# Eight graph convolutions on one core: the two chunks of a node pair moved by one transfer per stream

## Chip, cores and metric

The kernel runs on one core of a Trainium2 chip. The metric is the device time of one execution in microseconds (us). The engines are PE (matmul; PEld is its weight load), DVE (vector), ACT (scalar), POOL and SP; a trailing q (SPq, ACTq) marks work that the engine's sequencer does, such as issuing a transfer.

## What is computed

A chain of graph layers on 100,000 nodes of 128 features and 50,000 edges sorted by destination. Three GCN layers come first, then two EVE layers, two SAGE layers and one GAT layer; there are normalisations between them. All are gathers over the edges, a sum (or max) for each destination, and a matmul of every node row. The GCN layer, cut from the reference:

```python
loop = jnp.arange(N, dtype=src.dtype)
src2, dst2 = jnp.concatenate([src, loop]), jnp.concatenate([dst, loop])
deg = jax.ops.segment_sum(ew2, dst2, num_segments=N)
dinv = jnp.where(deg > 0, jax.lax.rsqrt(jnp.maximum(deg, 1e-12)), 0.0)
norm = dinv[src2] * ew2 * dinv[dst2]
msg = norm[:, None] * (x @ W)[src2]
out = jax.ops.segment_sum(msg, dst2, num_segments=N) + b
h = out + x0          # then relu (not after the last) and a batch norm over the nodes
```

An EVE layer is `x @ wself.T + eve @ weve.T + bias` with `eve` from the segment's max and min; a SAGE layer is `agg @ W_l.T + b + x @ W_r.T` with the segment's mean. The second layer of each ends in a residual sum with x0 and a layer norm.

## The kernel before

Node rows are cut into 98 chunks of 1024 rows (`CH`), 8 consecutive rows on each of 128 partitions (`T` = 8), so that a chunk is 512 KB with 4 KB on a partition. Two chunks make a node pair: 49 pairs, the last of 1024 and 672 rows. Edges are cut into chunks of 1024 too: 24 edge pairs and a rest.

The program is a row of phases with a barrier between them: constants and indices, then `Degrees` (trace time 89 to 893 us: adds up the degrees, writes rows scaled by dinv and fills the first table of sums with bias rows), the convolutions m0, m1, m2 (GCN, 893 to 5934), a normalisation of the nodes (5934 to 6499), m4 and m5 (EVE, 6499 to 10039), m6 and m7 (SAGE, 10039 to 13216), and the GAT layer (13216 to the end). m5 and m7 are the ones that add x0 and end in the layer norm.

In a convolution every engine runs its own copy of one order, `merged_sweep` (line 902): the unit of an edge pair, then the units of those node pairs whose destinations are complete, mostly two behind each edge pair (24 such bursts, with a first and a second unit). POOL does nothing but the edges' side: 392 indirect gathers (line 1070) and 392 indirect scatters (line 1078) in a convolution.

A node unit in class `Conv`:

- `load_nodes` (lines 1146 to 1171, SP): for every stream (the rows y, where there is one x0, and last the sums that the edges scattered) the two chunks, each by its own transfer into its own buffer with a semaphore of its own. The y transfer of chunk b waits until half b of the previous pair has been transposed and copied, the others until half b of their buffer has been used. There is one buffer for each chunk of a pair, so the next pair's chunk goes where this one's was. Two fills of the next table of sums with bias rows follow, from one row in SBUF.
- `turn_nodes` (PE, line 1187): 16 transposes, two banks a chunk, behind `have`, the wait for the chunk's y. `turned_to_sbuf` (ACT, line 1220) copies the four banks, `multiply_nodes` (PE, line 1205) multiplies them.
- `LinearNodes.vector` (EVE and SAGE; DVE, line 1772) adds the sums to the products into z, behind `have` for that chunk's sums. `GcnNodes.vector` adds x0 and sums into res_b (line 1669) and then the scaled products (line 1683) into acc.
- `finish_scalar` (ACT) makes the output of the previous pair, o or y1 (lines 1808, 759 and in GCN 1651); each chunk waits in `out_free` for the store of the same buffer a pair earlier. `store_before` and `store_pair` (line 1250) issue the two stores from ACT.

`Degrees` loads (line 1967), scales (ACT line 2062, DVE line 2095) and stores (ACT line 2070) in the same way, chunk by chunk, with the two fills (line 2074) behind the stores on ACT.

Of the kernel before, what the change touches and what calls it, by code (L numbers as in the profile page):

```python
# [82 lines left out]
def node_rows(t, c, sh):  # L83

    if isinstance(c, int) and c == sh.node_chunks - 1:
        part = t[0:sh.last_nodes, :]
    elif isinstance(c, int):
        part = t[sh.n - CH * (c + 1):sh.n - CH * c, :]
    else:
        part = t[bass.ds((sh.n - CH) - c * CH, CH), :]  # L90
    return part.rearrange("(p j) f -> p j f", j=T)

# [906 lines left out]
class Conv(Phase):  # L999
# [10 lines left out]
    def __enter__(self):  # L1010
# [20 lines left out]
        self.buf = {n: [self.sb(f"in_{n}{b}", [P, T, D]) for b in range(2)] for n in self.streams}  # L1031
        self.landed = {n: self.pair(f"landed_{n}") for n in self.streams}
# [4 lines left out]
        self.stored = self.pair("stored")  # L1037
# [108 lines left out]
    def load_nodes(self, sp, m, scattered):  # L1146


        for name in sorted(self.streams, key=lambda name: name == "sums"):
            for b in range(2):  # L1150
                c = m * 2 + b
                if name == "y":
                    sp.wait_ge(self.nodes_turned, 2 * m + b + 1)
                    sp.sem_inc(self.gate, 1)
                if name in self.used:
                    sp.wait_ge(self.used[name], 2 * m + b + 1)
                    sp.sem_inc(self.gate, 1)
                if name == "sums" and b == 0:
                    for s, n in enumerate(scattered):
                        if not isinstance(n, int) or n > 0:  # L1160
                            sp.wait_ge(self.scattered[s], 16 * T * n)
                            sp.sem_inc(self.gate, 1)
                sp.dma_start(self.buf[name][b][0:self.sh.rows(c), :, :],
                             node_rows(self.streams[name], c, self.sh)).then_inc(self.landed[name][b], 16)

        if self.fill_table is not None:
            for b in range(2):
                c = m * 2 + b
                n = self.sh.rows(c)
                sp.dma_start(node_rows(self.fill_table, c, self.sh),  # L1170
                             spread_slots(self.fill_row[0:n, :], [n, T, D])).then_inc(self.filled, 16)

    def all_filled(self, sp):
        if self.fill_table is not None:
            sp.wait_ge(self.filled, 16 * self.sh.node_chunks)

    def have(self, eng, name, m, b):
        eng.wait_ge(self.landed[name][b], 16 * m + 16)

    def turn_nodes(self, pe, m):  # L1180
        for i in range(4):
            n = self.sh.rows(m * 2 + i // 2)
            if i % 2 == 0:
                self.have(pe, "y", m, i // 2)
            pe.wait_ge(self.n_out_read, 4 * m + i + 1)
            for t in range(H):
                mm = pe.transpose(self.n_bank[i][:, t * P:t * P + n], self.buf["y"][i // 2][0:n, H * (i % 2) + t, :],  # L1187
                                  self.k["ident"][0:n, 0:n])
            mm.then_inc(self.n_turned, 1)

    def multiply_nodes(self, pe, m, weight, between=None, add=None):
        for i in range(4):
# [4 lines left out]
            if add:  # L1197
                if i % 2 == 0:
                    self.have(pe, add, m, i // 2)
# [35 lines left out]
    def store_before(self, act, m, out):  # L1235
        act.wait_ge(self.finished, 2 * m + 2)
        act.sem_inc(self.gate, 1)
        if isinstance(m, int):
            self.store_pair(act, m - 1, out)
        else:  # L1240
            with act.If(0 < m):
                self.store_pair(act, (m - 1).with_bounds(min_val=0), out)
            with act.Else():
                for b in range(2):
                    act.sem_inc(self.stored[b], 16)

    def store_pair(self, act, m, out):
        for b in range(2):
            c = m * 2 + b
            act.dma_start(node_rows(self.out_dram, c, self.sh), out[b][0:self.sh.rows(c), :, 0:D]).then_inc(self.stored[b], 16)  # L1250

    def out_free(self, eng, m, b):
        eng.wait_ge(self.stored[b], 16 * m + 16)

    def all_stored(self, eng):
        for b in range(2):
            eng.wait_ge(self.stored[b], 16 * self.sh.node_pairs + 32)
# [328 lines left out]
class GcnNodes:  # L1586
# [3 lines left out]
    def __init__(self, ph, no, scale_shift, next_scale_shift, as_rows):  # L1590
# [10 lines left out]
        self.y1 = [ph.sb(f"y1{b}", [P, T, D + 1]) for b in range(2)]  # L1601
# [7 lines left out]
        self.grants = [(ph.nodes_turned, 2)] + [(ph.used[n], 2) for n in ph.used] + [(s, 16) for s in ph.stored]  # L1609
# [35 lines left out]
    def finish_scalar(self, act, m):  # L1645
        ph = self.ph
        for b in range(2):
            n = ph.sh.rows((m - 1) * 2 + b)
            act.wait_ge(self.acc_done, 2 * m + b + 1)
            ph.out_free(act, m, b)  # L1650
            act.wait_ge(self.gram_done, 2 * m + 1)
            act.activation(self.y1[b][0:n, :, 0:D], self.acc[b][0:n, :, :], ACT.Copy if self.last else ACT.Relu).then_inc(ph.finished, 1)
        ph.store_before(act, m, self.y1)
# [4 lines left out]
    def vector(self, dve, m, scattered):  # L1658
        ph, k = self.ph, self.ph.k
        dve.wait_ge(ph.n_out_read, 4 * m + 4)  # L1660
        for b in range(2):
# [4 lines left out]
            ph.have(dve, self.res, m, b)  # L1666
            ph.have(dve, "sums", m, b)
# [63 lines left out]
class LinearNodes:  # L1731


    def __init__(self, ph, weight, finish):
        self.ph, self.weight, self.finish = ph, weight, finish
        self.z, self.o = ([ph.sb(f"{n}{b}", [P, T, D]) for b in range(2)] for n in ("z", "o"))
# [3 lines left out]
        self.grants = [(ph.nodes_turned, 2)] + [(ph.used[n], 2) for n in ph.used] + [(s, 16) for s in ph.stored]  # L1740
# [19 lines left out]
    def vector(self, dve, m, scattered):  # L1760
# [3 lines left out]
        for i in range(4):  # L1764
# [3 lines left out]
            ph.multiplied_node(dve, m, i)  # L1768
            if i % 2 == 0:
                ph.have(dve, "sums", m, b)  # L1770
# [25 lines left out]
    def finish_scalar(self, act, m):  # L1796
# [4 lines left out]
        for b in range(2):  # L1801
            n = ph.sh.rows((m - 1) * 2 + b)
            ph.out_free(act, m, b)
# [5 lines left out]
        ph.store_before(act, m, self.o)  # L1809
# [65 lines left out]
class Degrees(Phase):  # L1875
# [9 lines left out]
    def __enter__(self):  # L1885
# [9 lines left out]
        self.x = [self.sb(f"x{b}", [P, T, D]) for b in range(2)]  # L1895
        self.xs = [self.sb(f"xs{b}", [P, T, WIDE]) for b in range(2)]
# [9 lines left out]
        self.x_in, self.deg_in, self.stored = self.pair("x_in"), self.pair("deg_in"), self.pair("stored")  # L1906
# [6 lines left out]
    def grant(self, pool):  # L1913
        pool.sem_inc(self.deg_read, 1)
        for b in range(2):
            pool.sem_inc(self.low_scaled[b], 1)
            pool.sem_inc(self.high_scaled[b], 1)
            pool.sem_inc(self.stored[b], 16)
# [48 lines left out]
    def load(self, sp, m, scattered):  # L1967
# [6 lines left out]
        sp.sem_inc(self.gate, 1)  # L1974
        for b in range(2):
            c = m * 2 + b
            sp.dma_start(self.deg[0:sh.rows(c), b, :].unsqueeze(2), node_rows(self.dram["degree"], c, sh)).then_inc(self.deg_in[b], 16)
        for b in range(2):
            c = m * 2 + b
# [4 lines left out]
            sp.dma_start(self.x[b][0:sh.rows(c), :, :], node_rows(self.x_dram, c, sh)).then_inc(self.x_in[b], 16)  # L1984
# [67 lines left out]
    def node_scalar(self, act, m, scattered):  # L2052
# [4 lines left out]
        for b in range(2):  # L2057
            n = sh.rows(m * 2 + b)
            act.wait_ge(self.x_in[b], 16 * m + 16)
            act.wait_ge(self.stored[b], 16 * m + 16)  # L2060
# [3 lines left out]
        for b in range(2):  # L2064
            c = m * 2 + b
# [4 lines left out]
            act.dma_start(node_rows(self.out_dram, c, sh), self.xs[b][0:sh.rows(c), :, :]).then_inc(self.stored[b], 16)  # L2070
        for b in range(2):
            c = m * 2 + b
            n = sh.rows(c)
            act.dma_start(node_rows(self.fill_table, c, sh), spread_slots(self.fill_row[0:n, :], [n, T, D])).then_inc(self.filled, 16)

    def node_vector(self, dve, m, scattered):
        sh, k = self.sh, self.k
        for b in range(2):
            dve.wait_ge(self.deg_in[b], 16 * m + 16)
# [10 lines left out]
        for b in range(2):  # L2090
            n = sh.rows(m * 2 + b)
            dve.wait_ge(self.x_in[b], 16 * m + 16)
            dve.wait_ge(self.stored[b], 16 * m + 16)
# [8 lines left out]
def degrees(nc, k, dram, sh, x, out, fill):  # L2102
    with Degrees(nc, k, dram, sh, x, out, fill) as ph:
        with nc.Block() as block:
# [15 lines left out]
            def _(act):  # L2120
                act.wait_ge(ph.constants_set, 4)
                merged_sweep(act, k, sh, lambda *u: ph.scalar(act, *u), lambda *u: ph.node_scalar(act, *u), first_behind=3)
                for b in range(2):
                    act.wait_ge(ph.stored[b], 16 * sh.node_pairs + 16)
                act.wait_ge(ph.filled, 16 * sh.node_chunks)
# [566 lines left out]
```

## Time and profile before

| | us |
|---|---|
| median of 3 runs | 10869.92 |
| lowest and highest run | 10861.84, 10874.02 |
| the profiled execution, first to last instruction | 15443.7 |
| Degrees, in the trace | 804 |
| m0, m1, m2 (GCN), in the trace | 1665, 1690, 1686 |
| m4, m5 (EVE), in the trace | 1656, 1884 |
| m6, m7 (SAGE), in the trace | 1488, 1689 |

The profiled execution is 42% longer than the runs, which the prediction comes back to. A row of the timeline gives the start from the beginning of the span, the duration, the engine, the line and operation, the output and inputs, and for several alike in a row their count; in brackets the engine's idle time ahead of it and what ended it. Under --lines a group's row gives the count, the busy time, the mean of one, and its idle time by what ended it. The names leave buffer numbers out; m stands for all seven convolutions.

### The profile page before, as it was taken

What the parts mean: (1) busy time and instruction counts of PE and PEld (TensorE: products, weight loads), DVE (VectorE), ACT (ScalarE), POOL (GpSimd) and SP (SyncE); (2) the same over time, 40 slices, a digit from 0 to 9 for tenths busy, and PEclk for the clock granted to TensorE, in tenths of its full rate; (3) what the DMA queues carried; (4) which work ended last, traced back from release to release, by engine and by line L of the source; (5) the groups of instructions that cost most, each with busy time, mean ns of one, the idle gap of its engine ahead of it and who ended that gap; (6) DMA issues with size and microseconds to landing.
All of it is one profiled execution on the core that took longest, in us unless ns stands there. A gap on an engine that the chain in (4) does not pass through costs nothing. (4 is left out here: it accounts for less than half of the span.)

```text
span 15443.7 us, 165743 instructions
## 1 busy us (share of the span) xinstructions
PE 7253.9 (47%) x36946; PEld 5501.8 (36%) x36947; DVE 6203.1 (40%) x16108; ACT 4646.1 (30%) x8631; POOL 7180.1 (46%) x7582
## 2 busy tenths in 40 slices
PE   1024544454534448854455555533334445445553
PEld 0024444444534444333333333323333333223332
DVE  3333433343434335522222333322223333378887
ACT  1111111111211114422222333412223333266676
POOL 4654444444454441144444444355554444557663
PEclk9987777777767779977777777866666667667776
DMA  6965554666656667644444444545555555233333
GB/s 164 209 154 171 172 167 148 205 200 194 202 176 198 193 194 255 235 142 158 143 166 143 162 160 159 177 144 173 168 171 170 183 177 192 81 104 119 114 114 100
DMA packets 1864962, 2570.76 MB, mean 166 GB/s; under 512 B 255901, under 2 KB 1369141, under 8 KB 1864662
## 3 DMA queue, kind: packets, MB, share of 16 engines
q1 hardware_dynamic: 1134168, 1627.20, 32.9%
q10 hardware_dynamic: 504726, 564.87, 11.2%
q0 software_dynamic: 225792, 375.94, 8.7%
q14 instruction: 216, 1.77, 0.0%
q8 instruction: 60, 0.98, 0.0%
HBM read 1499.55 MB, written 1129.98 MB: 170 GB/s over the span
## 5 line engine op out<-in xcount | busy, mean ns | idle before, releaser
L1078 POOL DMA_INDIRECT sums_gcn<-m_result,m_idx x1176 | 1162.8, 989 | 2311.9 <-DVE m_result L1399 1952.8
L1220 ACT ACTIVATE m_nodeT<-m_n_bank 128x512 f32<-128x512 f32 x980 | 544.3, 597 | 4220.6 <-remote 2400.8
L1626 PE MATMUL m_gram<-m_y 128*128 128x129 f32 (+1 forms) x4800 | 900.6, 336 | 1765.6 <-issue 1462.9
L1683 DVE SCALAR_TENSOR_TENSOR m_acc<-m_n_bank,m_scales,m_res_b 128x128 f32<-128x128 f32 (+1 forms) x2352 | 644.9, 343 | 2569.6 <-remote 1864.2
L1078 POOL DMA_INDIRECT sums_eve<-m_result,m_idx x784 | 762.7, 973 | 1696.8 <-DVE m_result L1515 1470.9
L1187 PE MATMUL m_n_bank<-k_ident,m_in_y 128*128 128x128 f32 x5488 | 895.6, 321 | 1310.0 <-DVE m_z L1772 826.9
L1772 DVE TENSOR_TENSOR m_z<-m_n_bank,m_in_sums 128x512 f32<-128x512 f32 (+1 forms) x784 | 511.9, 687 | 2412.8 <-remote 1300.2
L1626 PEld LDWEIGHTS m_gram<-m_y 128*128 128x128 f32 (+1 forms) x4800 | 801.2, 245 | 1845.4 <-issue 1523.6
L1078 POOL DMA_INDIRECT sums_sage<-m_result,m_idx x784 | 762.7, 973 | 1375.9 <-DVE m_result L1399 1134.3
L1070 POOL DMA_INDIRECT m_rows<-node_rows_a,m_idx x1176 | 1124.4, 956 | 358.5 <-issue 338.1
L1187 PEld LDWEIGHTS m_n_bank<-k_ident,m_in_y 128*128 128x128 f32 x5488 | 754.1, 168 | 1437.8 <-DVE m_z L1772 902.7
L1222 ACT ACTIVATE m_nodeT<-m_n_bank,k_bn 128x512 f32<-128x512 f32 x392 | 285.9, 775 | 1931.9 <-PE m_n_bank L1187 1404.6
L1070 POOL DMA_INDIRECT m_rows<-node_rows_b,m_idx x784 | 749.6, 956 | 247.4 <-issue 231.5
L1205 PE MATMUL m_n_bank<-k_gcn,m_nodeT 128*128 128x128 f32 (+1 forms) x4704 | 696.0, 308 | 95.1 <-issue 64.2
L1201 PE MATMUL m_n_bank<-m_in_x,k_ident 128*128 128x512 f32 (+1 forms) x784 | 476.3, 693 | 558.9 <-ACT m_nodeT L1220 408.0
L1119 PE MATMUL m_e_turn<-k_ident,m_rows 128*128 128x128 f32 x2744 | 488.8, 309 | 483.1 <-DVE m_sums L1582 224.9
L2215 POOL DMA_INDIRECT sums_gat<-g_result,g_idx x392 | 441.0, 1125 | 578.3 <-DVE g_result L2509 465.8
L1205 PEld LDWEIGHTS m_n_bank<-k_gcn,m_nodeT 128*128 128x128 f32 (+1 forms) x4704 | 663.6, 223 | 117.2 <-issue 83.7
L1205 PE MATMUL m_n_bank<-k_self,m_nodeT 128*128 128x128 f32 x3136 | 472.3, 310 | 456.5 <-ACT m_nodeT L1220 396.3
L1205 PEld LDWEIGHTS m_n_bank<-k_self,m_nodeT 128*128 128x128 f32 x3136 | 464.0, 225 | 579.5 <-ACT m_nodeT L1220 405.6
L759 ACT ACTIVATE m_o<-m_z,m_ln_shift,m_ln_scale 128x128 f32<-128x128 f32 x1600 | 626.5, 479 | 94.0 <-DMA node_rows_c<-m_o 46.6
L1129 PE MATMUL m_e_out<-k_gcn,m_sums 128*128 128x128 f32 x2352 | 393.1, 319 | 514.0 <-DVE m_result L1399 423.6
(302 smaller groups left out, 17415.1 us busy)
## 6 DMA issues: line engine op xcount, KB each, us to landing
m_in_sums<-sums_gcn SPq DMA_DIRECT2D x291, 512.0 KB
m_in_y<-node_rows_a SPq DMA_DIRECT2D x291, 512.0 KB
sums_gcn<-k_gcn_b SPq DMA_DIRECT2D x194, 512.0 KB
node_rows_a<-m_y ACTq DMA_DIRECT2D x194, 512.0 KB
m_in_x<-in_x_dram SPq DMA_DIRECT2D x194, 512.0 KB
m_in_y<-node_rows_b SPq DMA_DIRECT2D x194, 512.0 KB
sums_eve<-k_eve_b SPq DMA_DIRECT2D x194, 512.0 KB
m_in_sums<-sums_eve SPq DMA_DIRECT2D x194, 512.0 KB
```

Of the source, the lines that this page charges most:

```text
L759: ins = act.activation(out[0:n, j, :], z[0:n, j, :], ACT.Identity, bias=self.shift[copy][0:n, at:at + 1], scale=self.scale[copy][0:n, at:a ...
L1070: pool.indirect_dma_start(self.rows[b][:, t, :], None, self.table[:, :], bass.IndirectOffsetOnAxis(self.idx[s][:, t:t + 1], 0)).then_inc(s ...
L1078: pool.indirect_dma_start(self.node_sums[:, :], bass.IndirectOffsetOnAxis(self.idx[s][:, T + t:T + t + 1], 0), self.result[b][:, t, :], No ...
L1119: mm = pe.transpose(bank[:, n * P:(n + 1) * P], self.rows[b][:, H * (i % 2) + n, 0:D], self.k["ident"][:, :])
L1187: mm = pe.transpose(self.n_bank[i][:, t * P:t * P + n], self.buf["y"][i // 2][0:n, H * (i % 2) + t, :], self.k["ident"][0:n, 0:n])
L1201: mm = pe.matmul(self.n_bank[i][0:n, :], self.k["ident"][0:n, 0:n], half.rearrange("p t f -> p (t f)"), start=True, stop=False)
L1205: mm = pe.matmul(self.n_bank[i][0:n, t * D:(t + 1) * D], self.nodeT[:, i, t * P:t * P + n], weight[:, :], start=not add, stop=not add or t ...
L1220: act.activation(out, src, ACT.Copy).then_inc(self.n_turn_read, 1)
L1626: mm = pe.matmul(self.gram[:, 0:D + 1], self.y1[b][0:rows[b], t, 0:D], self.y1[b][0:rows[b], t, :], start=False, stop=False, skip_group_ch ...
L1683: ins = dve.scalar_tensor_tensor(out=self.acc[b][0:n, tt, :], in0=ph.node_out(i, n)[:, t, :], scalar=self.scales[b][0:n, tt:tt + 1], in1=s ...
L1772: dve.tensor_tensor(self.z[b][0:n, half, :], ph.node_out(i, n), ph.buf["sums"][b][0:n, half, :], ALU.add).then_inc(ph.n_out_read, 1)
L2215: pool.indirect_dma_start(self.node_sums[:, :], bass.IndirectOffsetOnAxis(self.idx[s][:, T + t:T + t + 1], 0), self.result[b][:, t, :], No ...
```

## The change

The two chunk buffers of every stream, of the outputs and of the degree phase become halves of one tile with 16 slots. A pair's 2048 rows lie 16 to a partition (8 KB), and one transfer with one semaphore moves them: loads, fills and stores. The load waits until both halves are free; the readers wait once, for the whole pair; an output's buffer is free when the whole pair is stored. The last pair, with its shorter chunk, keeps two transfers a stream. The same rows are moved, the loops and the order on each engine stay, and the normalisation and the GAT phase aren't touched. In `Degrees` it is the same with the loads of degree and x, the store and the fill. The diff, cut to its core:

```diff
+def pair_rows_of(t, m, sh):
+    at = sh.n - 2 * CH * (m + 1) if isinstance(m, int) else bass.ds((sh.n - 2 * CH) - m * (2 * CH), 2 * CH)
+    part = t[at:at + 2 * CH, :] if isinstance(m, int) else t[at, :]
+    return part.rearrange("(p j) f -> p j f", j=2 * T)
...
-        self.buf = {n: [self.sb(f"in_{n}{b}", [P, T, D]) for b in range(2)] for n in self.streams}
-        self.landed = {n: self.pair(f"landed_{n}") for n in self.streams}
+        self.both = {n: self.sb(f"in_{n}", [P, 2 * T, D]) for n in self.streams}
+        self.buf = {n: [t[:, b * T:(b + 1) * T, :] for b in range(2)] for n, t in self.both.items()}
+        self.landed = {n: self.sem(f"landed_{n}") for n in self.streams}
...
-            for b in range(2):
-                c = m * 2 + b
-                if name == "y":
-                    sp.wait_ge(self.nodes_turned, 2 * m + b + 1)
-                    sp.sem_inc(self.gate, 1)
-                if name in self.used:
-                    sp.wait_ge(self.used[name], 2 * m + b + 1)
-                    sp.sem_inc(self.gate, 1)
...
-                sp.dma_start(self.buf[name][b][0:self.sh.rows(c), :, :],
-                             node_rows(self.streams[name], c, self.sh)).then_inc(self.landed[name][b], 16)
+            if name == "y":
+                sp.wait_ge(self.nodes_turned, 2 * m + 2)
+                sp.sem_inc(self.gate, 1)
+            if name in self.used:
+                sp.wait_ge(self.used[name], 2 * m + 2)
+                sp.sem_inc(self.gate, 1)
...
+            else:
+                sp.dma_start(self.both[name][:, :, :], pair_rows_of(self.streams[name], m, self.sh)).then_inc(self.landed[name], 16)
...
-    def have(self, eng, name, m, b):
-        eng.wait_ge(self.landed[name][b], 16 * m + 16)
+    def have(self, eng, name, m):
+        eng.wait_ge(self.landed[name], 16 * m + (32 if is_last(m, self.sh) else 16))
...
     def store_pair(self, act, m, out):
-        for b in range(2):
-            c = m * 2 + b
-            act.dma_start(node_rows(self.out_dram, c, self.sh), out[b][0:self.sh.rows(c), :, 0:D]).then_inc(self.stored[b], 16)
-
-    def out_free(self, eng, m, b):
-        eng.wait_ge(self.stored[b], 16 * m + 16)
+        if is_last(m, self.sh):
...
+        else:
+            act.dma_start(pair_rows_of(self.out_dram, m, self.sh), out[:, :, 0:D]).then_inc(self.stored, 16)
+
+    def out_free(self, eng, m):
+        eng.wait_ge(self.stored, 16 * m + 16)
```

## Rows read from the trace of the kernel before

**Rows 1.** The page's first line.

```profile
span 15443.7 us, 165743 instructions
```

**Rows 2.** Busy time by stage, m1, m4 and m6; columns in the first line.

```profile
core 0: us, PE busy (x) PEld busy (x) DVE busy (x) ACT busy (x) POOL busy (x), PEclk, DMA share, GB/s
2558.00:4248.00 1690.00, 812.77 (x5130) 742.87 (x5130) 649.58 (x1912) 311.96 (x394) 772.62 (x834) 0.72 0.60 193
6499.00:8155.00 1656.00, 840.05 (x4116) 616.11 (x4116) 433.41 (x492) 435.83 (x688) 766.32 (x834) 0.75 0.46 150
10039.00:11527.00 1488.00, 530.52 (x3528) 484.83 (x3528) 355.35 (x713) 337.95 (x394) 766.21 (x834) 0.67 0.52 167
```

**Rows 3.** Timeline of ACT and PE in m4, 7010 to 7040 us.

```profile
7011.15 3.29 PE L1187 MATMUL m_n_bank<-k_ident,m_in_y 128*128 128x128 f32 x16
...
7035.86 0.60 ACT L1220 ACTIVATE m_nodeT<-m_n_bank 128x512 f32<-128x512 f32 x1 [26.63 <-remote]
```

**Rows 4.** The page's costliest groups: ACT's copies of the turned rows.

```profile
L1220 ACT ACTIVATE m_nodeT<-m_n_bank 128x512 f32<-128x512 f32 x980 | 544.3, 597 | 4220.6 <-remote 2400.8
```

**Rows 5.** POOL by line in m4, 6499 to 8155 us.

```profile
L1078 POOL DMA_INDIRECT sums_eve<-m_result,m_idx x392 | 381.4, 973 | 739.0 <-DVE m_result L1515 626.1 <-issue 112.9
L1070 POOL DMA_INDIRECT m_rows<-node_rows_b,m_idx x392 | 374.8, 956 | 134.3 <-issue 118.4 <-PE m_e_turn L1119 9.8 <-DMA node_rows_b<-n_o 6.0
```

**Rows 6.** Timeline of one burst of m4, its second unit.

```profile
8082.37 1.17 SPq L1163 DMA_DIRECT2D m_in_y<-node_rows_b  x2
...
8086.29 0.99 ACTq L1250 DMA_DIRECT2D node_rows_a<-m_o  x2
...
8087.37 1.78 SPq L1163 DMA_DIRECT2D m_in_sums<-sums_eve  x2
...
8087.72 1.91 PE L1187 MATMUL m_n_bank<-k_ident,m_in_y 128*128 128x128 f32 x16
...
8093.07 1.06 ACT L1808 ACTIVATE m_o<-m_z 128x1024 f32<-128x1024 f32 x1 [1.68 <-DMA node_rows_a<-m_o]
...
8093.30 1.29 DVE L1772 TENSOR_TENSOR m_z<-m_n_bank,m_in_sums 128x512 f32<-128x512 f32 x2 [4.69 <-PE m_n_bank L1205]
...
8094.59 0.99 ACTq L1250 DMA_DIRECT2D node_rows_a<-m_o  x2
...
8095.06 1.29 DVE L1772 TENSOR_TENSOR m_z<-m_n_bank,m_in_sums 128x512 f32<-128x512 f32 x2 [0.47 <-DVE m_z L1772]
...
8096.09 0.69 ACT L1477 ACTIVATE m_mix<-m_pool,k_bconv 128x512 f32<-128x512 f32 x1 [1.96 <-PE m_pool L1440]
...
8099.59 1.28 DVE L1528 TENSOR_TENSOR_SCAN m_hi<-k_same_run,m_hi,m_pool 128x512 f32<-128x512 uint8 x1 [3.24 <-ACT m_pool L1496]
```

**Rows 7.** Timeline of one node unit of m1 (GCN).

```profile
4157.34 1.43 DVE L1669 TENSOR_TENSOR m_res_b<-m_in_x,m_in_sums 128x256 f32<-128x256 f32 x4
...
4158.76 1.42 DVE L1669 TENSOR_TENSOR m_res_b<-m_in_x,m_in_sums 128x256 f32<-128x256 f32 x4
...
4160.20 1.40 ACTq L1250 DMA_DIRECT2D node_rows_b<-m_y  x2
...
4163.96 2.16 DVE L1683 SCALAR_TENSOR_TENSOR m_acc<-m_n_bank,m_scales,m_res_b 128x128 f32<-128x128 f32 x8 [1.71 <-PE m_n_bank L1205]
```

**Rows 8.** Timeline of ACT in one unit of m5 (layer norm).

```profile
8673.19 0.99 ACTq L1250 DMA_DIRECT2D node_rows_c<-m_o  x2
...
8678.05 6.26 ACT L759 ACTIVATE m_o<-m_z,m_ln_shift,m_ln_scale 128x128 f32<-128x128 f32 x16 [0.97 <-DMA node_rows_c<-m_o]
```

**Rows 9.** Timeline of ACT in Degrees, one pair.

```profile
569.73 1.28 ACTq L2070 DMA_DIRECT2D scaled_rows<-deg_xs  x2
571.17 6.23 ACTq L2074 DMA_DIRECT2D sums_gcn<-k_gcn_b  x2
...
581.35 0.69 ACT L2062 ACTIVATE deg_xs<-deg_x,deg_dinv 128x128 f32<-128x128 f32 x2 [2.11 <-DMA scaled_rows<-deg_xs]
587.11 0.69 ACT L2062 ACTIVATE deg_xs<-deg_x,deg_dinv 128x128 f32<-128x128 f32 x2 [5.06 <-DMA scaled_rows<-deg_xs]
```

**Rows 10.** DMA queues in m1: packets, MB, share of 16 engines' time.

```profile
q1 hardware_dynamic: 150820, 230.52, 40.7%
q10 hardware_dynamic: 101566, 51.21, 10.3%
```

More of the change, by code:

```diff
@@ L1036, in __enter__ @@
         self.finished = self.sem("finished")
-        self.stored = self.pair("stored")
+        self.stored = self.sem("stored")
         self.filled = self.sem("filled")
@@ new lines, in load_nodes @@
+            if name == "sums":
+                for s, n in enumerate(scattered):
+                    if not isinstance(n, int) or n > 0:
+                        sp.wait_ge(self.scattered[s], 16 * T * n)
+                        sp.sem_inc(self.gate, 1)
+            if is_last(m, self.sh):
+                for b in range(2):
+                    c = m * 2 + b
+                    sp.dma_start(self.buf[name][b][0:self.sh.rows(c), :, :],
+                                 node_rows(self.streams[name], c, self.sh)).then_inc(self.landed[name], 16)
+            else:
+                sp.dma_start(self.both[name][:, :, :], pair_rows_of(self.streams[name], m, self.sh)).then_inc(self.landed[name], 16)
@@ L1739, in __init__ @@
             self.ln = Norm(ph, "ln", 2 * T)
-        self.grants = [(ph.nodes_turned, 2)] + [(ph.used[n], 2) for n in ph.used] + [(s, 16) for s in ph.stored]
+        self.grants = [(ph.nodes_turned, 2)] + [(ph.used[n], 2) for n in ph.used] + [(ph.stored, 16)]
     def tensor_start(self, pe):
@@ L1974, in load @@
         sp.sem_inc(self.gate, 1)
+        if is_last(m, sh):
+            for b in range(2):
+                c = m * 2 + b
+                sp.dma_start(self.deg[0:sh.rows(c), b, :].unsqueeze(2), node_rows(self.dram["degree"], c, sh)).then_inc(self.deg_in, 16)
+        else:
+            sp.dma_start(self.deg[:, :, :].rearrange("p b (t o) -> p (b t) o", o=1), pair_rows_of(self.dram["degree"], m, sh)).then_inc(self.deg_in, 16)
         for b in range(2):
[L1976 to L1979, printed above, removed]
             sp.wait_ge(self.low_scaled[b], m + 1)
@@ L1983, in load, with landed @@
             sp.sem_inc(self.gate, 1)
-            sp.dma_start(self.x[b][0:sh.rows(c), :, :], node_rows(self.x_dram, c, sh)).then_inc(self.x_in[b], 16)
+        if is_last(m, sh):
+            for b in range(2):
+                c = m * 2 + b
+                sp.dma_start(self.x[b][0:sh.rows(c), :, :], node_rows(self.x_dram, c, sh)).then_inc(self.x_in, 16)
+        else:
+            sp.dma_start(self.x_both[:, :, :], pair_rows_of(self.x_dram, m, sh)).then_inc(self.x_in, 16)
+    def landed(self, eng, sem, m):
+        eng.wait_ge(sem, 16 * m + (32 if is_last(m, self.sh) else 16))
     def tensor(self, pe, j, par, q, halves, back):
@@ L2064, in node_scalar @@
         for b in range(2):
-            c = m * 2 + b
             act.wait_ge(self.low_scaled[b], m + 2)
```

108 lines of the change are left out of this document (61 added, 47 removed).

## The prediction

> **What bounds the kernel now.** I began with the page's head. The profiled execution lasts 15443.7 us [rows 1], 42% more than the median of 10869.92, so the first question is where the 4574 us come from. The timeline shows it: in a burst of m4 PE ended its 16 transposes at 7011.15 + 3.29 = 7014.44, and ACT, which only has to copy them, began at 7035.86, after 26.63 us of idleness that no known engine or transfer ended ("remote") [rows 3]. Such waits in front of this one group add up to 2400.8 us [rows 4]. I take these stretches as belonging to the profiled execution alone. So I read costs from bursts that have no such hole, and carry them to the median as microseconds, not as a share.
>
> Next the stages. POOL's own work in m4 is 381.4 + 374.8 us of indirect transfers and 112.9 + 118.4 us of issue between them: 988 us, 41 us for each of the 24 bursts [rows 5]. Nothing in the change touches it, so 988 is a floor of a convolution. Taking some 22 us of hole out of each of 24 bursts (the idle 26.63 less some 4 us that a copy normally waits, an estimate of mine), m4 has 1656 - 528 = 1128 us of its own, m1 1690 - 528 = 1162, m6 1488 - 528 = 960 [rows 2]. So m4 and the GCN stages are above POOL's floor, and what delays their chain of node and edge units shows; m6 is at the floor, and there POOL hides a small delay.
>
> Third, the burst. In its second unit nothing is double buffered, so the loads are issued only when the first unit has let go of the buffers, and the reader: the trace shows y issued from 8082.37 to 8083.54 and transposed from 8087.72; the sums issued from 8087.37 to 8089.15 and used by DVE at 8093.30 and 8095.06; a store issued from 8086.29 to 8087.28, for whose second half ACT waits until 8093.07 [rows 6]. A transfer is home 4 to 6 us after its issue, and three of these are near the unit's path. That is where a single transfer for two chunks matters.
>
> **The change part by part.**
>
> *y, one transfer.* Its issue moves to where the second one is now; the first was issued up to 0.83 us earlier (1.17 us for both, a single one about 0.34). PE ran its 16 transposes in one go of 1.91 us [rows 6], so the second chunk had landed by 8087.72 + 0.95. The whole lands no earlier than the second chunk did: PE starts between 0 and 0.95 us later from that, plus up to the 0.83 us head start that the first chunk's bytes lose: 0 to 1.8. I take 1.3, above the middle, since the sums are delayed behind it too. The products wait for it, then m_pool, and ACT at 8096.09 waited for PE's m_pool [rows 6]: it is on the path.
>
> *sums, one transfer.* DVE's first z needs both chunks. The second z began at 8095.06, so the second chunk had landed by then: between 0 and 1.76 us later [rows 6]. The cover is the 3.24 us for which DVE waits ahead of its next edge operation, at 8099.59, on ACT [rows 6]: nothing shown beyond y's lateness. If that cover goes, 1.76 comes on top (the range has it).
>
> *Stores, one transfer.* ACT issues one where it issued two: half of 0.99 = 0.50 us less in a linear layer [rows 6], half of 1.40 = 0.70 in GCN [rows 7]. ACT's edge operation at 8096.09 came 0.51 us after the second store's issue ended (8094.59 + 0.99) [rows 6], so I give this back in full. Against it, output 0 now waits until the whole pair is stored. In m4 that output stands ahead of nothing late; in m5 and m7 it does: ACT's 16 norm applies of 6.26 us started after 0.97 us of waiting on the first half's store, and went on without a break, so the second half's store had landed by 8678.05 + 3.13 [rows 8]. The wait grows by 0.50 us (the second issue came that much later) up to 3.13; I take 1.5, near the lower end, since the two were issued side by side and share the same engines.
>
> *Net by stage.* m4: 24 x (1.3 - 0.5) = 19. m5 and m7: 24 x (1.5 - 0.5) = 24 each; y's lateness lies in PE's wait, off ACT's path there. m6: 0, under POOL's floor. GCN (m0 to m2): res_b's first half began at 4157.34, its second at 4158.76 without a break, so the sums come at most 1.42 us later; the third and fourth acc group waited 1.71 us for PE anyway, which covers it; y's 0.8 or so on PE stands against 0.70 less on ACT [rows 7]: 0.
>
> *Degrees.* ACT scales chunk 0 at 581.35 and chunk 1 at 587.11, each when its store is home [rows 9]. Now chunk 0 waits until about 587 as well: 0.69 us of ACT, at most 0.95 of DVE (not shown in these rows: an estimate from ACT's two of 0.69, as DVE scales six of eight slots), against half of 1.28 us of issue. ACT needs 6.23 us to issue two fills [rows 9]: the queue was full, and bytes, not waits, set the pace. I take 0, with up to 49 x 0.95 = 47 either way.
>
> *Fills, degree loads, last pair.* The fills have no reader in the phase: SP issues one fewer, 0. The last pair of a convolution has to wait for both chunks: 0.7 us (about one issue) x 7 = 5.
>
> **Sum:** 19 + 48 + 5 = 72 us, so 10869.92 + 72 = 10,942, 0.7% slower. The profiled execution would go from 15443.7 to about 15,516. With the upper ends everywhere it is m4 and m6 31 each (24 x 1.3), m5 and m7 63 each (24 x 2.63), Degrees 47, GCN 3 x 24 x 0.72 = 52, last pairs 5: 292, that is 11,162; with the lower ends 0 or a little less.
>
> **A rule to weigh.** Packets: in m1 q10 (the y1 stores, rows of 512 bytes) took 10.3% of 1690 us = 174 us for 51.21 MB, 3.4 us/MB; q1, with longer packets among its own, 40.7% = 688 us for 230.52 MB, 3.0 us/MB [rows 2, 10]. Per packet that is 27.4 and 73 ns of one engine for 504 and 1528 bytes: a fixed part of about 5 ns. If the 4 KB pieces of three loads (3 x 98 x 128 = 37,632 of them) become 8 KB, some 19,000 fewer packets in m1 save 19,000 x 5 / 16 = 6 us of DMA time; an estimate. The Trainium skill, page "DMA: Bandwidth & Descriptors", section "Rules for kernel authors", asks for 1 MiB or more in a DMA for the highest bandwidth, which would favour this change; here the rows leave 6 us a stage for it. The same skill's first page, "Trainium Kernel Development and Optimization", section "Best Practices", asks to double-buffer so that transfers overlap with compute, and the change makes one buffer of two: that speaks against it, and no row gives it a price of its own.
>
> **Rivals.**
>
> 1. *ACT's shorter queue decides (faster, 0.25).* If the loads are home in time with the whole pair (y late by under 0.5 us), the issues that ACT is spared remain: 24 x (3 x 0.70 + 4 x 0.50) = 98 us, 10,772; in all 49 pairs of a stage, not just the second of a burst, 49 x 4.1 = 201, 10,669. For it: the two chunks went out within 1.2 to 1.8 us and landed nearly together. Against it: PE and DVE wait for landings in the very burst, and ACT's wait at 8096.09 ended on PE, not on its own issue [rows 6]. It turns at 0.5 us of lateness on y.
>
> 2. *DMA engines decide (faster, 0.06).* In m1 they are busy for 0.60 x 1690 = 1014 us, 87% of the 1162 us without holes [rows 2]. Were they the limit, 6 us in each of 7 stages come off: 10,828. Against it: PE, not a transfer, is what the accumulation waits for [rows 7].
>
> 3. *No change (0.20).* POOL's 988 us floor hides it, if the convolutions without holes are nearer to the floor than my estimate: 10,870.
>
> 4. *Every landing shows (slower, 0.10).* The runs move the same bytes in 70% of the time, so queues are fuller. With y at 1.8 and sums at 1.76 both on the path, a burst pays 3.56 - 0.5 = 3.1 us in the four linear stages and 1.42 + 1.8 - 0.7 = 2.5 in GCN: 24 x (4 x 3.1 + 3 x 2.5) = 478, 11,348. Against it: DVE's 3.24 us of cover.
>
> **How the numbers follow.** My forecast has 0.39. About 0.2% (22 us) is what a measurement can tell from no change. Slower by more: 0.36 of the forecast and rival 4, 0.46. Within: rival 3 and 0.03 of the forecast's lower end, 0.23. Faster: rivals 1 and 2, 0.31. The range reaches up to the forecast's upper ends, 11,160, which leaves out most of rival 4, and down to 10,740, which leaves out rival 1's larger form: about 0.18 in all. Slower and faster both lie within it; the forecast's own range is 10,870 to 11,160.
>
> **What would show it.** In the new profile: one issue of y, sums and store in a burst; PE's transposes 5 to 6 us after y's issue; DVE's z (first) waiting on the sums' transfer instead of on PE; ACT's norm applies in m5 waiting 2 us or more on the store; POOL's scatters of m4 and m5 waiting somewhat longer for DVE. I am wrong if those waits are no longer than before, if ACT's edge operations begin earlier in a burst, or if the time went to Degrees.

## The result, and the profile after

The changed kernel takes 10986.44 us (median of 4 runs, 10974.47 to 11002.23), the kernel before 10865.88 in the same comparison: a ratio of 1.011, 95% interval 1.0095 to 1.0124. That is 1.1% slower; forecast were 0.7%, in a range that holds it. The sum came out roughly, the terms did not: the stages that were to pay did not, and those that were to be even paid nearly all of it.

The first line of the changed kernel's page (it answers to [rows 1]):

```profile
span 10972.6 us, 158031 instructions
```

This profiled execution lasts as long as the runs do. To compare stage by stage, the kernel before was profiled once more, unchanged; that execution took 10876.9 us, so the holes of its first profile (15443.7 us) were indeed that one execution's own. All comparisons below are with this second profile, named *before (second)*. Its busy times by stage (Degrees, m0, m1, m2, m4, m5, m6, m7):

```profile
core 0: us, PE busy (x) PEld busy (x) DVE busy (x) ACT busy (x) POOL busy (x), PEclk, DMA share, GB/s
89.00:888.00 799.00, 48.04 (x392) 45.24 (x392) 276.96 (x646) 141.39 (x295) 463.86 (x442) 1.00 0.88 203
888.00:1941.00 1053.00, 715.93 (x5134) 666.20 (x5134) 651.51 (x1914) 216.15 (x345) 777.58 (x834) 0.85 0.80 262
1941.00:3003.00 1062.00, 708.21 (x5130) 655.81 (x5130) 652.13 (x1911) 312.08 (x394) 779.54 (x834) 0.87 0.90 307
3003.00:4073.00 1070.00, 729.36 (x5134) 678.76 (x5134) 653.09 (x1915) 313.16 (x394) 778.10 (x834) 0.85 0.91 304
4638.00:5660.00 1022.00, 755.68 (x4116) 537.96 (x4116) 432.02 (x492) 436.48 (x688) 766.23 (x834) 0.91 0.72 243
5660.00:6852.00 1192.00, 933.22 (x4508) 604.25 (x4508) 646.02 (x1627) 658.85 (x1438) 766.19 (x834) 0.92 0.73 252
6852.00:7874.00 1022.00, 495.40 (x3528) 474.66 (x3528) 354.94 (x713) 335.59 (x394) 766.26 (x834) 0.75 0.71 243
7874.00:8918.00 1044.00, 709.37 (x3920) 570.87 (x3920) 570.16 (x1848) 560.40 (x1144) 766.36 (x834) 0.80 0.82 287
```

The same stages of the changed kernel:

```profile
89.00:932.00 843.00, 48.09 (x392) 45.30 (x392) 269.30 (x646) 136.54 (x295) 463.43 (x442) 1.00 0.80 193
932.00:2000.00 1068.00, 725.03 (x5134) 681.56 (x5134) 647.64 (x1914) 212.89 (x345) 783.21 (x834) 0.86 0.80 258
2000.00:3085.00 1085.00, 711.83 (x5130) 666.85 (x5130) 646.06 (x1911) 308.69 (x394) 789.02 (x834) 0.85 0.90 300
3085.00:4170.00 1085.00, 718.16 (x5134) 672.35 (x5134) 646.70 (x1915) 308.27 (x394) 785.53 (x834) 0.85 0.89 300
4735.00:5758.00 1023.00, 741.95 (x4116) 540.97 (x4116) 431.70 (x492) 435.48 (x688) 766.26 (x834) 0.91 0.71 243
5758.00:6944.00 1186.00, 929.88 (x4508) 604.74 (x4508) 644.92 (x1627) 660.12 (x1438) 766.14 (x834) 0.93 0.71 253
6944.00:7970.00 1026.00, 488.58 (x3528) 471.56 (x3528) 353.04 (x713) 335.70 (x394) 766.10 (x834) 0.74 0.71 242
7970.00:9017.00 1047.00, 689.92 (x3920) 562.62 (x3920) 569.74 (x1848) 561.28 (x1144) 766.29 (x834) 0.81 0.81 286
```

The first number behind the stretch is the stage's length. Degrees is 44 us longer, and its share of DMA time fell from 0.88 to 0.80: the transfers did not get dearer (0.88 x 799 = 703 us of busy time before, 0.80 x 843 = 674 now), they stood still more often. The GCN stages are 15, 23 and 15 us longer. m4, m6 and m7 are within 4 us, and m5 is 5 to 6 us shorter. Together with single microseconds elsewhere that is the difference of the two spans, 96 us; the medians differ by 121.

Why m4 did not move is in POOL's scatters, *before (second)* and the changed kernel:

```profile
L1078 POOL DMA_INDIRECT sums_eve<-m_result,m_idx x392 | 381.3, 973 | 126.7 <-issue 115.5 <-DVE m_result L1515 7.8 <-DMA sums_eve<-m_result,m_idx 2.1
```

```profile
L1091 POOL DMA_INDIRECT sums_eve<-m_result,m_idx x392 | 381.3, 973 | 127.1 <-issue 116.4 <-DVE m_result L1536 8.0 <-DMA sums_eve<-m_result,m_idx 2.4
```

In the first profile POOL waited 626.1 us here for DVE's results [rows 5]; without the holes it is 7.8. By the prediction's sum (gathers, scatters and the issue between them) POOL works 983 us of m4's 1022: m4 was near POOL's floor all the time, and what its node units lose is hidden. They do lose: PE's waits for y grew by 41 us, DVE's for the sums by 84. Each row has the sum in us, the number and the longest, *before (second)* and changed:

```profile
DVE m_z L1772 <- DMA m_in_sums<-sums_eve: 105.1, 27, 16.4
...
PE m_n_bank L1187 <- DMA m_in_y<-node_rows_b: 72.6, 33, 10.1
```

```profile
DVE m_z L1799 <- DMA m_in_sums<-sums_eve: 188.8, 22, 17.5
...
PE m_n_bank L1207 <- DMA m_in_y<-node_rows_b: 114.0, 26, 12.1
```

In m5 it is another matter. There POOL does wait for DVE's results, about once in every burst, and yet the change did not lengthen these waits:

```profile
POOL sums_eve L1078 <- DVE m_result L1515: 171.9, 22, 22.3
```

```profile
POOL sums_eve L1091 <- DVE m_result L1536: 165.7, 22, 23.2
```

### The profile page after: what moved, and what is told of

Same layout as the page of the kernel before. It is cut to its first block and busy times, and to the rows that moved or that the text cites. A ratio compares the mean times of both kernels' runs of the same rounds, so it can differ in the third digit from the quotient of the medians.

```text
span 10972.6 us, 158031 instructions
## 1 busy us (share of the span) xinstructions
PE 6691.1 (61%) x36946; PEld 5130.0 (47%) x36947; DVE 6177.8 (56%) x16108; ACT 4620.5 (42%) x8631; POOL 7254.6 (66%) x7582
## 5 line engine op out<-in xcount | busy, mean ns | idle before, releaser
L1207 PE MATMUL m_n_bank<-k_ident,m_in_y 128*128 128x128 f32 x5488 | 829.4, 311 | 906.9 <-DMA m_in_y<-node_rows_c 386.1
L1207 PEld LDWEIGHTS m_n_bank<-k_ident,m_in_y 128*128 128x128 f32 x5488 | 722.8, 162 | 977.7 <-issue 800.0
L1648 PE MATMUL m_gram<-m_y 128*128 128x129 f32 (+1 forms) x4800 | 739.6, 325 | 451.4 <-ACT m_y L1675 450.6
L1648 PEld LDWEIGHTS m_gram<-m_y 128*128 128x128 f32 (+1 forms) x4800 | 711.3, 238 | 478.9 <-ACT m_y L1675 478.6
L1967 POOL DMA_INDIRECT degree<-deg_deg_slot,deg_place_slot x392 | 452.2, 1154 | 359.6 <-DVE deg_deg_slot L2054 250.4
L771 ACT ACTIVATE m_o<-m_z,m_ln_shift,m_ln_scale 128x128 f32<-128x128 f32 x1600 | 626.4, 479 | 129.3 <-DMA node_rows_c<-m_o 76.3
L1132 PEld LDWEIGHTS m_e_turn<-k_ident,m_rows 128*128 128x128 f32 x2744 | 375.3, 161 | 625.1 <-DVE m_sums L1603 181.7
L1225 PE MATMUL m_n_bank<-k_gcn,m_nodeT 128*128 128x128 f32 (+1 forms) x4704 | 584.6, 278 | 0.0
L1225 PEld LDWEIGHTS m_n_bank<-k_gcn,m_nodeT 128*128 128x128 f32 (+1 forms) x4704 | 561.6, 195 | 0.0
L1070 POOL COPY m_idx<-k_edge_idx 128x16 int32 (+1 forms) x350 | 71.9, 208 | 722.3 <-POOLq L118 696.3
L2248 POOL DMA_INDIRECT g_src_rows<-node_rows_b,g_idx x392 | 445.7, 1137 | 112.7 <-issue 112.7
```

The lines of the kernel that those rows point to most:

```text
L771: ins = act.activation(out[0:n, j, :], z[0:n, j, :], ACT.Identity, bias=self.shift[copy][0:n, at:at + 1], scale=self.scale[copy][0:n, at:a ...
L1132: mm = pe.transpose(bank[:, n * P:(n + 1) * P], self.rows[b][:, H * (i % 2) + n, 0:D], self.k["ident"][:, :])
L1225: mm = pe.matmul(self.n_bank[i][0:n, t * D:(t + 1) * D], self.nodeT[:, i, t * P:t * P + n], weight[:, :], start=not add, stop=not add or t ...
L1648: mm = pe.matmul(self.gram[:, 0:D + 1], self.y1[b][0:rows[b], t, 0:D], self.y1[b][0:rows[b], t, :], start=False, stop=False, skip_group_ch ...
L1967: pool.indirect_dma_start(self.dram["degree"][:, :], bass.IndirectOffsetOnAxis(self.place_slot[s][:, t:t + 1], 0), self.deg_slot[b][:, t:t ...
```

## The experiments

All stage lengths are read from the barriers of each run's trace, one profile for each kernel. "GCN" is m0, m1 and m2 together. The ratio is to the kernel before in the same comparison. Code that a run leaves as it is gives a measure of chance: such stages differ between two profiles by up to 4 us in Degrees, 11 in GCN and 12 in m5.

| kernel | Degrees | GCN | m5 | median | ratio to before (95%) |
|---|---|---|---|---|---|
| before (second) | 799 | 3185 | 1191 | 10878.75 (one run) | |
| changed | 843 | 3238 | 1186 | 10986.44 | 1.011 (1.0095 to 1.0124) |
| Degrees alone | 847 | 3177 | 1203 | 10928.02 | 1.0045 (1.0032 to 1.0059) |
| convolutions alone | 798 | 3227 | 1193 | 10932.85 | 1.0050 (1.0036 to 1.0064) |
| pair waits, chunk transfers | 863 | 3233 | 1239 | 11026.49 | 1.013 (1.0113 to 1.0147) |
| stores by chunk | 785 | 3199 | 1190 | 10877.35 | 1.0001 (0.9991 to 1.001) |
| loads by chunk | 824 | 3265 | 1250 | 11050.81 | 1.016 (1.0143 to 1.0177) |
| both by chunk | 787 | 3193 | 1215 | 10929.40 | 1.0047 (1.0031 to 1.0064) |
| stores by chunk, wait by pair | 778 | 3237 | 1225 | 10955.06 | 1.0084 (1.0069 to 1.01) |
| two late stores in Degrees | 844 | 3231 | 1187 | 10976.56 | 1.0101 (1.0085 to 1.0116) |
| one fill in Degrees | 794 | 3186 | 1190 | 10872.34 | 0.9999 (0.999 to 1.0008) |
| early stores | 797 | 3170 | 1162 | 10842.75 | 0.9975 (0.9966 to 0.9984) |
| paired loads, early stores | 779 | 3195 | 1213 | 10908.13 | 1.0023 (1.001 to 1.0036) |

**Which half of the change pays.** Three runs: the kernel before again, the change in `Degrees` alone, and in the convolutions alone. In the two mixed ones the row order of the table of dinv differs between its writer and the GCN stages, so a GCN row is scaled by another row's dinv and the values are not the layer's; the work is the same.

> The kernel before, unchanged, for a second profile of it. Theory A (the convolutions pay, Degrees is even): without the holes of the first profile Degrees takes 820 to 860 us, as in the changed kernel (842), and m4 and m5 together are some 40 to 60 us shorter than the changed kernel's 1023 and 1186. Theory B (Degrees pays): Degrees takes 730 to 780 us and the convolutions are within 10 us each of the changed kernel's.

> Only Degrees has pair transfers, the convolutions move each chunk by itself. Theory A (the convolutions pay): within 0.2% of the kernel before, 10,850 to 10,890 us. Theory B (Degrees pays: with the whole pair behind one load and one store, a pair's load, scaling and store follow one another): 10,930 to 10,990 us, most of the 120 us.

> Only the convolutions have pair transfers, Degrees moves each chunk by itself. Theory A: 10,930 to 10,990 us. Theory B: 10,850 to 10,900 us. If the two parts add up, this and the run with Degrees alone have excesses that sum to about 120 us.

Each half costs about half a per cent: 0.45% and 0.50%, whose sum, 0.95%, is at the edge of the interval of the whole. Neither theory holds alone, and Degrees before, 799 us, lies in neither's range. The stages say more: with Degrees alone that stage takes 847 us and GCN is no longer than before (3177); m5 is 12 us longer there, though that run changes nothing in it. With the convolutions alone GCN is 42 us longer and Degrees is as before (798).

**Waiting or transfer?** The waits of the change with the transfers of before:

```diff
-            if is_last(m, self.sh):
+            if True:
                 for b in range(2):
...
-        eng.wait_ge(self.landed[name], 16 * m + (32 if is_last(m, self.sh) else 16))
+        eng.wait_ge(self.landed[name], 32 * m + 32)
```

(fills, stores and `Degrees` alike; in `Degrees` both stores still leave only when both halves are scaled)

> Two transfers per stream as before (512 KB, 8 rows per partition), but issued together and waited for as a pair, as in the change. Theory W (the coarser waits cost the time): Degrees 830 to 860 us, m0 to m2 together 3,220 to 3,250, total 10,960 to 11,000. Theory T (one long transfer is the cost, by its 8 KB rows or its landing): Degrees 790 to 810, m0 to m2 3,180 to 3,195, total 10,860 to 10,890.

1.3% slower, Degrees 863, GCN 3233: theory W in the stages, in the sum 26 us above its range. It is the change's coarser waiting that costs, not the long transfer. Whether one transfer in place of two gives a little back (11026 against 10986) is not shown: the two intervals overlap, and most of the 40 us lie in m5 (1239 against 1186) and Degrees.

**Loads or stores?** On the 16-row layout of the change, first the stores, then the loads, then both go by chunk again, with a semaphore for each (in `Degrees` a chunk's store then leaves, as before the change, as soon as its half is scaled):

```diff
-            act.dma_start(pair_rows_of(self.out_dram, m, self.sh), out[:, :, 0:D]).then_inc(self.stored, 16)
+        for b in range(2):
+            n = self.sh.rows(m * 2 + b)
+            act.dma_start(half_rows_of(self.out_dram, m, b, self.sh), out[0:n, b * T:(b + 1) * T, 0:D]).then_inc(self.stored[b], 16)
```

> The change with the stores alone undone: 16 rows per partition, one load per pair, but each chunk's 8 rows of a partition stored by a transfer and a semaphore of its own. Theory S (the wait for the whole pair's store costs): Degrees back to 795 to 810 us and m0 to m2 to 3,180 to 3,200, total 10,870 to 10,890. Theory L (the single load costs): Degrees 835 to 850, m0 to m2 3,220 to 3,245, total 10,960 to 10,990.

> The change with the loads alone undone: each chunk's 8 rows of a partition loaded by a transfer and a semaphore of its own as soon as its half is free, stores by pair. Theory L: Degrees 795 to 810 us, m0 to m2 3,180 to 3,200, total 10,870 to 10,890. Theory S: Degrees 835 to 850, m0 to m2 3,220 to 3,245, total 10,960 to 10,990. If both share, each of this run and the one before lies near the middle, about 10,920.

> The 16-row layout kept, loads and stores both by chunk with a semaphore each (4 KB pieces of 8 KB rows); only the fills and the load of the degrees stay by pair. Theories W, L and S: as the kernel before, 10,855 to 10,890 us, Degrees 790 to 810. If the layout of rows itself costs (another stride in memory): 10,920 or more.

It is mainly the stores. With them by chunk the time is that of before (1.0001), although every load is still one transfer. That evenness is a sum of two parts: Degrees is 14 us shorter than before (785), GCN 14 longer (3199), so of the 53 us that GCN lost 39 came back; the rest is little above the 11 us of chance. With the loads by chunk and the stores by pair it is slower than the change, 1.6%, which theory S didn't expect: m5 takes 1250 us there. Both by chunk is 0.5% slower than before, mostly in m5 (1215) and in the GAT layer, which is 28 us longer in that profile although nothing of it was changed. Beside the run with stores by chunk alone, a pair's load on this layout is then no loss, and 4 KB pieces out of 8 KB rows may be one. I can't say more of it.

**What about the stores: their waits?** To the run with stores by chunk only this is added:

```diff
-            ph.out_free(act, m, b)
+            if b == 0:
+                ph.out_free(act, m, 0)
+                ph.out_free(act, m, 1)
```

and the same for ACT and DVE in `Degrees`.

> The run with stores by chunk (10,877 us) with one thing put back: the writers of an output wait for both chunks' stores before they write the first half; the transfers stay two. Theory S1 (the wait for the whole pair costs, not the size of the store): Degrees 825 to 850 us, m0 to m2 together 3,225 to 3,260, total 10,950 to 11,010. Theory S2 (the single long store costs): Degrees 780 to 795, m0 to m2 3,190 to 3,210, total 10,870 to 10,890.

The two places part. GCN goes from 3199 to 3237, the changed kernel's 3238 (2, 19 and 17 us in m0, m1 and m2): there it is the wait for both stores (S1), and one store in place of two is worth nothing. Degrees goes to 778, less than with a wait for each: there it is neither. m5 goes to 1225, which S1 doesn't explain, as the changed kernel has the same wait and 1186.

How the wait costs GCN, in m1. Waits of ACT for the store and of PE for ACT, *before (second)*, then changed:

```profile
ACT m_y L1652 <- DMA node_rows_b<-m_y: 159.9, 45, 6.2
PE m_gram L1626 <- ACT m_y L1652: 147.7, 56, 13.4
```

```profile
PE m_gram L1648 <- ACT m_y L1675: 173.3, 45, 14.3
...
ACT m_y L1675 <- DMA node_rows_b<-m_y: 138.6, 23, 8.7
```

ACT waits no longer in sum, but before a wait was 3.6 us in the mean, ahead of a single half; now it is 6.0 us ahead of both. PE, which multiplies y1 by itself in the middle of its node unit, gets the first half later: 173.3 us instead of 147.7. This reaches POOL only where POOL has to wait for edge results. POOL's scatters in m1: *before (second)*, changed, stores by chunk, stores by chunk with the pair wait:

```profile
L1078 POOL DMA_INDIRECT sums_gcn<-m_result,m_idx x392 | 388.2, 990 | 145.7 <-issue 116.1 <-DVE m_result L1399 27.5 <-DMA sums_gcn<-m_result,m_idx 1.8
```

```profile
L1091 POOL DMA_INDIRECT sums_gcn<-m_result,m_idx x392 | 395.1, 1008 | 158.1 <-issue 117.1 <-DVE m_result L1420 40.2 <-DMA sums_gcn<-m_result,m_idx 0.9
```

```profile
L1098 POOL DMA_INDIRECT sums_gcn<-m_result,m_idx x392 | 389.3, 993 | 143.6 <-issue 117.1 <-DVE m_result L1426 25.0 <-DMA sums_gcn<-m_result,m_idx 1.5
```

```profile
L1098 POOL DMA_INDIRECT sums_gcn<-m_result,m_idx x392 | 391.1, 998 | 165.9 <-issue 116.7 <-DVE m_result L1426 47.1 <-DMA sums_gcn<-m_result,m_idx 2.1
```

For the kernels of 1062 and 1067 us POOL waits 27.5 and 25.0 us for results, for those of 1085 and 1086 it is 40.2 and 47.1, in three to five waits, the long ones (7 to 19 us) in the last 91 us of the stage. For most of the stage the delay is hidden behind POOL's queue; it is paid at the end, where the last edge pairs stand behind node units that take longer. In the changed kernel that is 12.7 of 23 us; most of the rest is POOL's own busy time, 789.02 us instead of 779.54, which has no cause here: the run with the pair wait, with 781.47, is as slow.

**What about the stores in Degrees?** In the run of 778 us the first store goes out once its half is scaled, in the changed kernel once both are. This run splits the changed kernel's store but issues both pieces late:

```diff
-            act.dma_start(pair_rows_of(self.out_dram, m, sh), self.xs_both[:, :, :]).then_inc(self.stored, 16)
+            for b in range(2):
+                act.dma_start(half_rows_of(self.out_dram, m, b, sh), self.xs[b][:, :, :]).then_inc(self.stored, 16)
```

> The changed kernel; only in Degrees the pair's store is split into two transfers, both issued where the one was, once both halves are scaled, and waited for together. In the run with a store for each chunk and pair waits, Degrees took 778 us, but there the first store left about 0.9 us earlier. Theory E (the earlier issue of the first store is the gain): Degrees 825 to 850 us as in the changed kernel, total 10,970 to 11,000. Theory Z (the long store itself lands late): Degrees 775 to 790, total 10,910 to 10,940. The convolutions are those of the changed kernel: m0 to m2 3,225 to 3,250.

844 us: theory E. The size of the store is nothing (843 and 844), the moment of its issue 66 us (778 to 844). The other runs agree: wherever the first store waits until the second half is scaled too, Degrees takes 824 to 863 us, wherever it doesn't, 778 to 799. One pair of Degrees, the changed kernel and then the run of 778 us:

```profile
594.53 1.28 ACT L2101 ACTIVATE deg_xs<-deg_x,deg_dinv 128x128 f32<-128x128 f32 x4 [5.09 <-DMA deg_x<-in_x_dram]
...
596.82 0.33 SPq L2019 DMA_DIRECT2D deg_x<-in_x_dram  x1
596.98 0.36 ACTq L2115 DMA_DIRECT2D scaled_rows<-deg_xs  x1
```

```profile
589.56 1.28 ACT L2112 ACTIVATE deg_xs<-deg_x,deg_dinv 128x128 f32<-128x128 f32 x4 [6.26 <-DMA deg_x<-in_x_dram]
...
591.05 1.12 ACTq L2119 DMA_DIRECT2D scaled_rows<-deg_xs  x2
591.94 0.33 SPq L2028 DMA_DIRECT2D deg_x<-in_x_dram  x1
```

From the start of scaling to the first store it is 2.45 us against 1.49, and the next pair's 1 MB load is issued 0.16 us ahead of the store in the one, 0.89 us behind it in the other. Over the stage the load goes ahead of the first store in 29 of 48 pairs of the changed kernel and of the run with two late stores, in none of the run of 778 us. Then the waits of ACT in Degrees, for the store and for x: *before (second)*, changed, two late stores, and the run of 778 us:

```profile
ACT deg_xs L2062 <- DMA scaled_rows<-deg_xs: 121.2, 39, 7.3
...
ACT deg_xs L2062 <- DMA deg_x<-in_x_dram: 47.9, 27, 5.5
```

```profile
ACT deg_xs L2101 <- DMA scaled_rows<-deg_xs: 273.4, 29, 16.4
...
ACT deg_xs L2101 <- DMA deg_x<-in_x_dram: 93.0, 20, 7.5
```

```profile
ACT deg_xs L2109 <- DMA scaled_rows<-deg_xs: 314.0, 33, 20.3
...
ACT deg_xs L2109 <- DMA deg_x<-in_x_dram: 82.1, 16, 8.4
```

```profile
ACT deg_xs L2112 <- DMA deg_x<-in_x_dram: 166.6, 32, 13.4
...
ACT deg_xs L2112 <- DMA scaled_rows<-deg_xs: 121.4, 17, 13.8
```

Where the store leaves late, the wait for it more than doubles, up to 20 us a piece, and the DMA engines are less busy: a share of 0.80 in the changed kernel and 0.79 with two late stores, 0.83 in the run of 778 us. That the loss is more than the 0.96 us of issue (66 / 49 = 1.35 us a pair) fits the load's place ahead of the store, but no run moved the load alone, so that part is not shown.

**One fill.** The kernel before, with only the two fills of a pair in `Degrees` merged. Before, ACT's 98 issues of them took 156 us, up to 6.4 us one, the changed kernel's 50 only 29.

> The kernel before with one piece of the change alone: in Degrees the two fills of a pair are one transfer. Theory F (ACT stood in the issue of the second fill, 156 us in 98 issues, as the queue was full; a single one goes in at once): Degrees 780 to 790 us instead of 799, the rest as before, total 10,850 to 10,868. Theory N (the transfers set the pace there, so that the issue costs nothing): Degrees 795 to 802, total within 0.1% of the kernel before.

0.9999, Degrees 794, a microsecond under N's range and four above F's: theory N within the noise. The time that ACT no longer spends in the issue it spends in waiting for the store instead (213.5 us, where *before (second)* has 121.2).

**Earlier stores.** If late stores cost, earlier ones may gain. In the kernel before each chunk's store is moved right behind its own output:

```diff
-        ph.store_before(act, m, self.o)
+            ph.store_before(act, m, self.o, b)
```

(inside the loop over the two chunks; the same with `self.y1`), with the parts of Degrees that had given 778 us, but on rows of 8 to a partition.

> The kernel before with, in Degrees, one load of x and one fill per pair, two stores as each half is scaled, and waits for both stores (the parts that gave 778 us), and in the convolutions each chunk's store issued right behind its own output instead of behind both. If the wait for the stores is what is left to gain in GCN (160 us of ACT's time in m1 before): Degrees 775 to 790, m0 to m2 together 3,130 to 3,175 instead of 3,185, m5 1,170 to 1,190, total 10,780 to 10,850. If the transfers themselves set the pace of GCN (0.90 of the DMA engines' time): m0 to m2 unchanged within 10, total 10,845 to 10,865.

0.9975 (0.9966 to 0.9984), 10,843 us: faster than both kernels by its interval. m5 is 29 us shorter, GCN 15. The first expectation holds in GCN (3170) and in the sum, and m5 is shorter still than it said. Degrees was missed by both: 797, not 778; its x loads, of 4 KB pieces, made ACT wait 249 us, where the run of 778 us has 166.6. So the 8 KB rows may be worth some of the 778; no run changed them alone. Hence the last run, which keeps the change's loads and fills and stores early by chunk:

> The change with its loads and fills by pair kept and its stores alone undone: a transfer and a semaphore for each chunk, issued as soon as that half is written (in Degrees the writers wait for both stores, as in the run with 778 us). If the parts add up: Degrees 775 to 785 us, m0 to m2 together 3,170 to 3,190, m5 1,155 to 1,170, total 10,815 to 10,845, some 0.4% under the kernel before. If the early stores give nothing beside paired loads: m0 to m2 about 3,199 as in the run with stores by chunk, m5 1,190, total 10,865 to 10,880.

The parts don't add up: 1.0023, outside both ranges. Degrees gives 779 as expected, but GCN is 3195 and m5 1213: beside paired loads the earlier stores gave nothing in the convolutions. Why is open. The best version measured is the run before it.

## Why the prediction was right, and where it was not

- *The first profile's holes.* That they belong to that execution alone was right. Their size was not: I took 22 us for each of 24 bursts out of m1, m4 and m6 alike, and got 1162, 1128 and 960 us of their own [rows 2]; the second profile has 1062, 1022 and 1022. The 960 for m6 was a sign: it lies under the 988 that were called a floor. The wait row of one engine at one place was not enough to price a burst. From this came the wrong ranking of the stages: m4 seemed 140 us above POOL's floor of 988, and was 34.
- *m4, 19 us: 1.* The mechanism is there (y and sums are waited for 41 and 84 us longer in the stage; 41 over 24 bursts are 1.7 each, where 1.3 was taken), but hidden by POOL. The step that failed is "So m4 and the GCN stages are above POOL's floor" for m4. m6 at the floor was right.
- *m5 and m7, 24 each: -5 and +3.* ACT's wait for the store in m5 did grow, from 51.5 us in 33 waits to 76.3 in 25. One wait is 1.5 us longer, which is what I took, but there are fewer of them: 25 us over 24 bursts are 1.0 each. It did not lengthen the stage, and POOL's queue did not hide it either, as POOL waits for DVE there once a burst (171.9 us before, 165.7 changed). The step that failed is that this wait lies on the stage's path; what covers it is open.

The rows for this, *before (second)* and changed:

```profile
ACT m_o L759 <- DMA node_rows_c<-m_o: 51.5, 33, 2.5
```

```profile
ACT m_o L771 <- DMA node_rows_c<-m_o: 76.3, 25, 7.4
```

- *GCN, 0: 53 us.* The step that failed is "y's 0.8 or so on PE stands against 0.70 less on ACT". I left out of GCN the wait that I priced in m5: y1's first half behind the whole pair's store. There PE waits for y1 in the middle of its node unit. The runs with stores by chunk, without and with the pair wait (3199, 3237), show that this wait is 38 of the 53 us; 14 stayed with stores by chunk.
- *Degrees, 0 with 47 either way: 44.* "The queue was full, and bytes, not waits, set the pace" failed: DMA's share fell to 0.80. I took account of chunk 0's wait, but not of the first store, which leaves about a microsecond later in a pair. That 44 is close to the 47 is chance: the 47 priced the wait, and with the same wait and an earlier store the stage takes 778 us.
- *Rival 1.* ACT's spared issues are real, and worth nothing measurable: in GCN one store and two, both waited for as a pair, give 3238 and 3237 us, and in Degrees 50 fills in place of 98 give 0.9999.
- *Rival 2.* The rule that transfers of 1 MiB or more move data fastest (the Trainium skill, "DMA: Bandwidth & Descriptors", "Rules for kernel authors") is not shown at work here. Degrees' DMA busy share times length fell from 703 to 674 us, but with two stores of half the length, in the run of 778 us, it is lower still (0.83 x 778 = 646). In m1 it rose: 0.90 x 1062 = 956, 0.90 x 1085 = 977.
- *Rivals 3 and 4.* That POOL's floor hides the change (rival 3) is what happened in m4 and m6, not in the whole; that every landing shows (rival 4) did not happen.
- *The signs.* The waits for y, for the sums and for the store grew as foretold, POOL's scatters in m4 and m5 did not wait longer (7.8 and 8.0 us in m4). And "if the time went to Degrees" was one of my signs of being wrong: 44 of the 96 us did.

The sum was within the range because the missed Degrees and GCN (97 us) took the place of m4, m5 and m7 (67 us): a good part of that is luck. The 5 us for the last pairs were not measured by themselves. The cause named, a wait for two halves of a single buffer, is the one that the runs show in GCN, for the output's buffer, which was not priced there. In Degrees it is another, the later issue of the store.

## What to carry to other kernels

Before a stage's cost is multiplied by the number of bursts, find what sets its floor: here a queue of indirect transfers hid the delays of m4 and m6, and in m1 let them through at the end of the stage. Merging transfers into one also merges their waits and their moments of issue, and here these cost more than the merging gave: for the output's buffer in GCN it was the wait, in Degrees the moment. Merged loads cost nothing in the sum (1.0001). To issue each store as soon as its piece is written gained 0.25% on the layout of before, and nothing in the convolutions beside merged loads, so each combination has to be measured. And a profile that is 42% longer than the runs should be taken again before stages are ranked by it.

## What was not expected of the hardware

Two fills of 512 KB issued one behind the other held ACT's queue up to 6.4 us for one issue, a single fill of 1 MB, with the same bytes, at most 1.0 (1.4 in the run with one fill); on the path this was worth nothing. Where the first of two stores was issued about a microsecond later, often behind a 1 MB load on another queue, the pair took 1.35 us longer. And m5 stays open: it took between 1162 and 1250 us in these kernels, 1186 with all transfers by pair, 1225 with stores by chunk and the pair wait, 1250 with loads by chunk and stores by pair. Two profiles of the same code differ there by 12 us, and no theory here orders these numbers.
